# A selective-scan network on one core: the C guest matmul with 128 columns, the look-ahead normalisation spread over thirty steps, the token-major B guests divided

## The reference

```python
xz = h @ in_w
xs, z = jnp.split(xz, 2, axis=-1)
xs = jax.nn.silu(xs)
proj = xs @ xproj_w
dt = jax.nn.softplus(proj[..., :D_INNER] + dt_bias)
Bm = proj[..., D_INNER:D_INNER + D_STATE]
Cm = proj[..., D_INNER + D_STATE:]
A = -jnp.exp(A_log)
...
dA = jnp.exp(dt_t[:, :, None] * A)
hst = hst * dA + (dt_t * x_t)[:, :, None] * B_t[:, None, :]
y_t = jnp.einsum('bds,bs->bd', hst, C_t)
...
y = jnp.swapaxes(ys, 0, 1) + xs * Dskip
return y * jax.nn.silu(z) @ out_w
```

## Time and profile before

| | us |
|---|---|
| median of 3 runs | 3326.49 (3325.43 to 3328.09) |
| the profiled execution's own time | 3327.19 |
| its span in the trace | 3325.4 |
| busy: PE / DVE / ACT / POOL | 3211.2 / 2775.5 / 2801.9 / 2516.3 |
| prologue, to the first scan instruction | 69.5 |
| the 128 steps of the first batch | 629.4 |
| from them to the first scan instruction of the second batch | 188.0 |
| direction 0 of the second batch | 316.4 |
| direction 1 of the second batch | 314.4 |

### The profile page before, as it was taken

The page is one execution under the profiler, slowest core; times in us unless marked ns, Lnnn a source line. Parts: engine busy times, 40 slices in busy tenths (PEclk is TensorE's granted clock), DMA queues, the critical chain, the costliest instruction groups (busy, mean ns, idle before and its releaser), DMA issues.

```text
span 3325.4 us, 60434 instructions
## 1 busy us (share of the span) xinstructions
PE 3211.2 (97%) x23656; PEld 2670.8 (80%) x23656; DVE 2775.5 (83%) x2969; ACT 2801.9 (84%) x4968; POOL 2516.3 (76%) x1120
## 2 busy tenths in 40 slices
PE   8999999999899999999989999999999999999999
PEld 7989898974698988996468999899637898888854
DVE  3999999966399999996549999999555999999962
ACT  4999999955599999994569999999457999999744
POOL 3999999950299999993039999999305999999800
PEclk9999999999999999999999999999999999999999
DMA  4211212200212111120021121212002222111100
GB/s 164 71 66 52 74 52 72 65 32 1 77 55 66 67 65 63 61 69 22 1 86 58 66 69 56 71 53 71 13 1 86 64 66 65 57 58 58 39 13 7
DMA packets 57900, 187.19 MB, mean 56 GB/s; under 512 B 6664, under 2 KB 12808, under 8 KB 56848
## 3 DMA queue, kind: packets, MB, share of 16 engines
q1 hardware_dynamic: 57616, 183.33, 16.3%
HBM read 180.14 MB, written 3.16 MB: 55 GB/s over the span
## 4 chain that ended last, share of the span: by engine, by line
PE 65%; POOL 17%; ACT 8%; issue 7%; DVE 2%; DMA 1%; SPq 0%; DVEq 0%; ACTq 0%; POOLq 0%
POOL states L567 16%; PE bank L977 16%; PE bank L959 13%; PE bank L960 8%; PE bank L855 7%; ACT decay L710 4%; PE bank L1176 4%; PE bank L1049 3%; ACT inflow_tok L704 3%; PE bank L1095 2%; PE bank L1197 2%; PE bank L1276 2%; PE bank L1209 2%; DVE states L1413 1%; PE bank L1030 1%
## 5 line engine op out<-in xcount | busy, mean ns | idle before, releaser
L567 POOL TENSOR_TENSOR states<-states,c_rows 128x1024 f32<-128x1024 f32 x1020 | 2390.2, 2389 | 440.0 <-DMA c_rows<-c_spill 389.5
L1413 DVE TENSOR_TENSOR_SCAN states<-decay,bank 128x512 f32<-128x512 f32 x2048 | 2357.0, 1204 | 196.7 <-ACT decay L710 147.9
L710 ACT ACTIVATE decay<-dt,a_log 128x512 f32<-128x512 f32 x2048 | 1307.6, 714 | 0.0
L977 PE MATMUL bank<-ident,states 128*128 128x128 f32 x8192 | 1240.9, 274 | 30.2 <-POOL states L567 6.6
L959 PE MATMUL bank<-ident,inflow_tok 128*128 128x128 f32 x6144 | 1034.4, 277 | 31.7 <-DVE states L1413 16.0
L704 ACT ACTIVATE inflow_tok<-dtx_tok,b_tok 128x512 f32<-128x512 f32 x1536 | 995.9, 715 | 42.3 <-PE bank L960 39.1
L977 PEld LDWEIGHTS bank<-ident,states 128*128 128x128 f32 x8192 | 951.8, 141 | 71.3 <-POOL states L567 63.3
L959 PEld LDWEIGHTS bank<-ident,inflow_tok 128*128 128x128 f32 x6144 | 714.2, 141 | 190.9 <-issue 98.4
L960 PE MATMUL bank<-b_diag,dtx_tok 128*128 128x128 f32 x4096 | 792.4, 275 | 0.0
L960 PEld LDWEIGHTS bank<-b_diag,dtx_tok 128*128 128x128 f32 x4096 | 619.0, 191 | 0.0
L705 ACT ACTIVATE b_diag<-ident,b_tok 128x128 f32<-128x128 f32 x512 | 201.1, 393 | 0.0
(11 more groups left out here) (154 smaller groups left out, 1975.0 us busy)
## 6 DMA issues: line engine op xcount, KB each, us to landing
c_rows<-c_spill SPq DMA_DIRECT2D x256, 512.0 KB, 3.7
xproj_w<-in_xproj_w SPq DMA_DIRECT2D x32, 320.0 KB, 4.2
in_w<-in_in_w SPq DMA_DIRECT2D x16, 512.0 KB, 4.8
in_w<-in_fc_w SPq DMA_DIRECT2D x8, 512.0 KB, 5.3
xproj_w<-in_w SPq DMA_DIRECT2D x8, 512.0 KB, 5.1
xproj_w<-in_fc_w SPq DMA_DIRECT2D x4, 1024.0 KB, 4.8
x_ahead<-in_x SPq DMA_DIRECT2D x4, 512.0 KB, 5.2
y_gated<-in_mod_w SPq DMA_DIRECT2D x4, 512.0 KB, 8.3
```

The costliest lines, as they stand in the source:

```text
L567: pool.tensor_tensor(pair, pair, c_row, ALU.mult).then_inc(weighed, 1)
L710: act.activation(decay[:, r % SLOTS * KI + k, :], dt[:, d, k, :], ACT.Exp, scale=a_neg[:, d, k, s:s + 1]).then_inc(decay_ready, 1)
L977: last = pe.matmul(banks[KI + t][:, k * P:(k + 1) * P], states[:, r % SLOTS * KI + k, t * P:(t + 1) * P], ident[:], is_transpose=True, sta ...
L1413: dve.tensor_tensor_scan(states[:, slot, time], decay[:, slot, time], banks[k % INFLOW_BANKS][:, time], 0.0, ALU.mult, ALU.add).then_inc(s ...
```

## The change

Four things change, in the tables and in `prepare` and `look_ahead`:

1. The C guest takes `xproj_w[:, kc, DI:DI + 2 * NS]` as weights, B and C together, 128 columns where it had 64, and writes all 128 partitions of `guest[0]`. C is then on partitions 64 to 127, and `c_t`, its copy and its spill to DRAM use these partitions.
2. The B guests are divided: two of the four matmuls of a step after tile 1, two after tile 3.
3. The look-ahead is spread: statistics at steps 8, 9, 11, 13 (were 8 to 11), aggregation at 14 (12), variance at 16 (13), power at 17 (14), normalisations at 19, 24, 29, 36 (16 to 19), transposes at 57 and 58 (22 and 27), shifts at 59 and 60 (24 and 29).
4. The waits follow: the transposes at 57 wait for the copies of the current `dtx`, the first input guest of the next direction waits for the new `h_ssm`, and the waits for `h_ssm` in the dt guests are gone.

```diff
--- before.py
+++ after.py
@@ -78,13 +78,13 @@
 B_COPY_AT = 48
 DTX_TURN_AT = (47, 49, 51, 53)
 DTX_COPY_AT = (49, 51, 53, 55)
-AHEAD_STATS_AT = (8, 9, 10, 11)
-AHEAD_AGGR_AT = 12
-AHEAD_VAR_AT = 13
-AHEAD_POWER_AT = 14
-AHEAD_NORM_AT = (16, 17, 18, 19)
-AHEAD_TURN_AT = (22, 27)
-AHEAD_SHIFT_AT = (24, 29)
+AHEAD_STATS_AT = (8, 9, 11, 13)
+AHEAD_AGGR_AT = 14
+AHEAD_VAR_AT = 16
+AHEAD_POWER_AT = 17
+AHEAD_NORM_AT = (19, 24, 29, 36)
+AHEAD_TURN_AT = (57, 58)
+AHEAD_SHIFT_AT = (59, 60)
 EPS_MAMBA = 1e-5
 EPS_LN = 1e-6
 EPS_NORM = 1e-12
@@ -178,7 +178,7 @@
         x_att = x_ssm
         x_out = x_mlp
 
-        c_t = sb("c_t", [NS, L])
+        c_t = sb("c_t", [P, L])[NS:2 * NS, :]
         dtx_tok = sb("dtx_tok", [P, 2, TT, DI])
         inflow_tok = sb("inflow_tok", [P, SLOTS, TT - 1, DI])
         y_gated = sb("y_gated", [P, 2, KI, L])
@@ -441,7 +441,7 @@
             def spill(n):
 
                 sp.wait_ge(c_t_ready, n + 1)
-                sp.dma_start(c_spill[n:n + 1].rearrange("a m h (j l) -> (a m h j) l", l=L), c_t[:]).then_inc(c_spilled, 16)
+                sp.dma_start(c_spill[n:n + 1].rearrange("a m h (j l) -> (a m h j) l", l=L), c_t).then_inc(c_spilled, 16)
 
             def spread_rows(b, r):
 
@@ -855,7 +855,7 @@
                     out = pe.matmul(to[:, c], lhs, rhs[:, c], start=start and half == 0, stop=stop, skip_group_check=True)
                 return out
 
-            def prepare(n, d, s, h=(0, 1), ahead=None, first=False):
+            def prepare(n, d, s, h=(0, 1), first=False):
 
                 if s in IN_AT:
                     at = IN_AT.index(s)
@@ -871,6 +871,9 @@
                             pe.wait_ge(h_high_ready, 1)
                         else:
                             pe.wait_ge(dtx_tok_ready, n * KI)
+                            if n % 2 == 0:
+                                pe.wait_ge(h_low_ready, n // 2 + 1)
+                                pe.wait_ge(h_high_ready, n // 2 + 1)
                     elif kc == 0:
 
                         pe.wait_ge(in_ready, n * 2 * KI + m - 1)
@@ -886,7 +889,7 @@
                     if kc == 0 and 0 in h:
                         pe.wait_ge(xproj_loaded, 16 * KI * (n + 1))
                         pe.wait_ge(in_ready, n * 2 * KI + 2 * KI - 1)
-                    last = halves(guest[0][0:NS, :], xproj_w[:, kc, DI + NS:DI + 2 * NS], xs[:, kc, :], h, kc == 0, kc == KI - 1)
+                    last = halves(guest[0], xproj_w[:, kc, DI:DI + 2 * NS], xs[:, kc, :], h, kc == 0, kc == KI - 1)
                     if kc == KI - 1 and 1 in h:
                         last.then_inc(c_mm, 1)
                 for m in range(KI):
@@ -895,29 +898,25 @@
                         if kc == 0 and 0 in h:
                             if m == 0:
                                 pe.wait_ge(in_ready, (n + 1) * 2 * KI)
-                                if ahead is not None:
-                                    pe.wait_ge(h_low_ready, ahead)
                             elif m == 1:
                                 pe.wait_ge(c_t_ready, n + 1)
-                                if ahead is not None:
-                                    pe.wait_ge(h_high_ready, ahead)
                             else:
                                 pe.wait_ge(dt_ready, n * KI + m - 1)
                         last = halves(guest[(m + 1) % 2], xproj_w[:, kc, m * P:(m + 1) * P], xs[:, kc, :], h, kc == 0,
                                       kc == KI - 1)
                         if kc == KI - 1 and 1 in h:
                             last.then_inc(dt_mm, 1)
+                if s in B_TOK_AT:
+                    t = B_TOK_AT.index(s)
+                    if t == 0 and 0 in h:
+                        pe.wait_ge(dt_ready, n * KI + KI - 1)
+                    for kc in [2 * half + i for half in h for i in range(2)]:
+                        last = pe.matmul(guest[1][:, t * NS:(t + 1) * NS], xs[:, kc, t * P:(t + 1) * P],
+                                         xproj_w[:, kc, DI:DI + NS], start=(kc == 0), stop=(kc == KI - 1), skip_group_check=True)
+                    if t == TT - 1 and 1 in h:
+                        last.then_inc(b_tok_mm, 1)
                 if 0 not in h:
                     return
-                if s in B_TOK_AT:
-                    t = B_TOK_AT.index(s)
-                    if t == 0:
-                        pe.wait_ge(dt_ready, n * KI + KI - 1)
-                    for kc in range(KI):
-                        last = pe.matmul(guest[1][:, t * NS:(t + 1) * NS], xs[:, kc, t * P:(t + 1) * P],
-                                         xproj_w[:, kc, DI:DI + NS], start=(kc == 0), stop=(kc == KI - 1))
-                    if t == TT - 1:
-                        last.then_inc(b_tok_mm, 1)
                 if s in DTX_TURN_AT:
                     k = DTX_TURN_AT.index(s)
                     pe.wait_ge(dtx_ready, n * KI + k + 1)
@@ -937,12 +936,8 @@
                     f = AHEAD_TURN_AT.index(s)
                     if f == 0:
                         pe.wait_ge(ahead_norm, (b + 1) * TT)
-                    if n is not None:
-
-                        if f == 0:
-                            pe.wait_ge(in_ready, (n + 1) * 2 * KI)
-                        else:
-                            pe.wait_ge(c_t_ready, n + 1)
+                        if n is not None:
+                            pe.wait_ge(dtx_tok_ready, (n + 1) * KI)
                     for t in range(TT):
                         last = pe.transpose(guest[1 - f][:, t * P:(t + 1) * P], x_norm[:, t, f * P:(f + 1) * P], ident[:])
                     last.then_inc(ahead_turned, 1)
@@ -1001,7 +996,7 @@
                     if k % 2 and s in SKIP_AT:
                         skip_term(d, SKIP_AT.index(s), k // 2)
                     if k % 2 and (d == 0 or not last):
-                        prepare(b * 2 + d + 1, 1 - d, s, (k // 2,), b + 2 if d == 0 and not last else None)
+                        prepare(b * 2 + d + 1, 1 - d, s, (k // 2,))
                     if d == 1 and s in Y_TURN_AT and k == 1:
                         turn_low(b, Y_TURN_AT.index(s))
                     if d == 1 and s in PROJECT_AT and k % 2:
@@ -1368,7 +1363,7 @@
                     dve.scalar_tensor_tensor(to, part[:, m % KI, :], 1.0, guest[m % 2], ALU.add, ALU.mult).then_inc(in_ready, 1)
                 if s == C_COPY_AT:
                     dve.wait_ge(c_mm, n + 1)
-                    dve.tensor_copy(c_t[:], guest[0][0:NS, :]).then_inc(c_t_ready, 1)
+                    dve.tensor_copy(c_t, guest[0][NS:2 * NS, :]).then_inc(c_t_ready, 1)
                 if s in DT_CAP_AT:
                     k = DT_CAP_AT.index(s)
                     dve.wait_ge(dt_mm, n * KI + k + 1)
```

## The result

The changed kernel takes 3311.08 us (median of 5 runs, 3308.55 to 3313.58) against 3327.86 (median of 5, 3325.43 to 3328.47): ratio 0.9949, 95% interval 0.9937 to 0.996. That is 16.8 us less by the medians and 18.6 by the profiled executions (3308.55 against 3327.19); forecast were 20.7 and a time of 3306.

What follows compares the result with a forecast made beforehand. No single engine bounded the whole; each step had its own, with GpSimd's floor 4.66 us. Savings 8.2 + 0.3 + 11.7 + 0.5 = 20.7 from 3327.2 gave 3306.5, from the median 3305.8: 3306 us, own range 3302 to 3310, wider 3299 to 3314.

Steps and rivals of the forecast that it cites:

- The C guest, 2.05 a sequence: Steps 20 to 23: 128 columns avoid the shape change, 21.6 to 19.5 us; 8.2 over four sequences without look-ahead.
- the second rival: Wide C guest does not reach the dt guest's pace: 3315 us, or 3322 with longer weight loads; chance 0.07 for both.
- The shape change in the prologue, 0.3: In the prologue the array's shape changes once and back; avoiding this saves 0.3 us.
- The copy of `c_t`, "nothing either way": Copy and spill move the same values from other partitions: no effect, bounded by 0.1 us for seven.
- Steps 17 to 54 at GpSimd's 186.1: Direction 0 with look-ahead: GpSimd becomes the bound, 186.1 us against 184.2 otherwise; 3.5 us gained from 189.6.
- The account's start: GpSimd's work in steps 17 to 54, 188.0 us, counted from no backlog at the stretch's start, up to 1.85 at its end.
- The first rival: GpSimd does not bind in direction 0 and the B gain is kept: 3298 us, chance 0.12.
- the third: Rival: spread normalisations at 24, 29 and 36 meet `dtx`, each putting its 1.2 us on the path: 3320 us, chance 0.06.
- Steps 10 and 12, 0.6: Direction 0 with look-ahead: these steps lose their statistics of 0.3 us beside a tanh step; gain 0.6.
- Moved transposes and shift, 0.2: Moved into steps 57 to 60 they cost 0.2 us per direction with look-ahead, bounds 0 and 1.5.
- the slower rival: TensorE waits at step 57 or direction 1's start and the scan stands: 3348 us at three steps; chance 0.02.
- B guests, 0.5 for all: In the other four directions 0.5 us won at steps 44 and 45 is given back; 0.5 taken for all.

Runs made afterwards that it cites:

- e1: Changed kernel with C's 64 columns laid in front of B's in xproj_w, so C comes out on partitions 0 to 63: 3309.41 us.
- e3: Changed kernel with GpSimd's four look-ahead normalisations writing one column instead of 256 for batches 1 to 3, work left out: 3303.39 us.
- e2: Changed kernel with the C guest back at 64 columns on partitions 0 to 63: 3319.55 us.
- e4: Changed kernel with the four B matmuls of a step back behind tile 1: 3312.04 us.
- e6: Changed kernel with normalisations together at steps 16 to 19 and statistics, aggregation, variance and power earlier: 3311.46 us.
- e7: Changed kernel with the edits of e1 and the look-ahead earlier, normalisations at steps 13, 16, 20 and 29: 3303.48 us.

## Why the prediction was right, and where it was off

The range of 3299 to 3314 held, and the forecast's mechanism is the one found; the sum was 3.9 us too large by the medians, 2.1 by the profiled executions. The median of 3311.1 is 5.1 over the forecast: 3.9 by the sum, and most of the rest because the kernel before measured 3327.9 this time, 1.4 more than when the forecast was made. It lies outside the forecast's own 3302 to 3310, and the wider range reached it only by allowing for rivals of which none came true. That much of the hit is luck.

- **The C guest, 2.05 a sequence.** Right: 21.61 to 19.55. The 0.29 of a guest was the change of shape, and the weight loads, longer by 56 ns, cost nothing, so the second rival is out. In the last batch's direction 0 it is 1.9; its step 20 takes 5.03, and why was not tried.
- **The shape change in the prologue, 0.3.** Right by the distances of its matmuls, 0.33. The whole prologue can't show it: over the ten traces it takes between 68.1 and 70.3 us.
- **The copy of `c_t`, "nothing either way".** Wrong: it was bounded by 0.1 for all seven, and by no row. Step 25 is 0.27 longer in each of seven sequences; e1 got back 0.3 in four directions and under 0.1 in three, 1.4 in all. The rule of the Trainium skill (VectorE: DVE Perf Modes, Two Vector instructions with no wait between them) covers this copy and could have been read beforehand.
- **Steps 17 to 54 at GpSimd's 186.1.** 186.4. GpSimd was busy for 186.0 of it, as the account had it; the rest is idle time of 0.43 in steps 17 and 18, ahead of the power, which the account did not have. The path of TensorE and VectorE, put at 184.2, is at most the 184.6 of e3, with the copy's 0.27. That GpSimd would take the place of both was the likeliest case and e3 shows it. The first rival, no bound by GpSimd, is out; so is the third, since waits of 1.8 us are far from the 4.8 of all normalisations in full.
- **The account's start.** It counts from GpSimd's last idle moment: step 18 in the changed kernel, one step into the stretch, which is why the account came out there; step 24 in e2, where it did not.
- **One batch read for three.** Steps 17 to 54 before the change took 189.6 in the second batch, which was read, and 189.3 in the first and third.
- **Steps 10 and 12, 0.6.** 0.59, at 5.07 each now.
- **Moved transposes and shift, 0.2.** Steps 57 and 59 grew by 0.2 and 0.5, and steps 60 to 62 gave back 0.5: steps 55 to 63 are 0.2, 0.2 and 0.04 longer. No wait at step 57 or at the start of direction 1 appeared, and the slower rival is out with it.
- **B guests, 0.5 for all.** 0.7 by direction 1 of e4 against the changed kernel (0.1, 0.2, 0.5). Given back by step 54, as said.
- **The rest.** The steps account for 18.1 us, the terms of the sum for 20.4 there. Of the 2.3 between them 1.1 is the copy in the four directions without look-ahead, and 1.5 the stretch in the three with it: 0.9 (three times 0.3) over 186.1, and 0.6 from the two batches that were shorter before. B gave 0.2 more than forecast; the rest is tenths. That the medians differ by 16.8 and not by 18.6 is within the scatter of single runs.

## What to carry to other kernels

Before moving work between steps, keep an account for each engine that runs near the pace: where it was last idle, what it must do from there, and how far it may fall behind. Work is free only if it lies where the account has slack: spread over a stretch that has none, the normalisations gained nothing over a block that starts three steps earlier (e6), and spread and moved to where there is slack they gained 1.2 us a batch (e7 against e1). A matmul with fewer output columns in a stream of full ones can be made full where, as here, the change of the array's shape costs more than the unused columns, and its result should come out on the partitions that the engine behind it works on (e1). A stage may give back what another wins before the scan ends, so read the gain some steps further on. And read a stretch in every batch before multiplying it by three.

## What the runs showed of the hardware

- Going from 128x128 to 128x64 and back cost TensorE 0.29 us each time, while a run of 64-column matmuls went at the same 0.216 us apiece as the 128-column ones in the changed kernel's prologue; the extra lay at the changes, 0.09 ahead of the pair, 0.05 within it and 0.15 behind it.
- A VectorE copy on partitions 64 to 127 between scans on 0 to 127 started 0.115 us later, and let the next scan start 0.144 later, than the same copy on partitions 0 to 63, in every one of its seven places in the scans.
- One of ten traces had ScalarE's decay and inflow products at 728 ns instead of 714, each of some 3600, with no effect on the steps that e1, at 713, shows.
